# Last context rows in fp32 over four column groups inside the queries, and a new order of the ramp, in a one-core Perceiver block

## The reference

```python
x = x + xattn(layernorm(x), ctx, ctx, Wq, Wk, Wv, Wo)
# in xattn:
q = (query @ Wq)          # 1024 rows x 1024
k = (key @ Wk)            # 32 x 257 rows x 256
v = (value @ Wv)          # 32 x 257 rows x 256
scores = q @ k.T * 32 ** -0.5          # per batch and head
out = softmax(scores) @ v
return out @ Wo
```

## Time and profile before

| what | us |
|---|---|
| median of three runs | 1087.92 (1085.78 to 1088.8) |
| the profiled execution, and its span | 1086.56, 1085.0 |
| PE busy | 1053.6 (97% of the span) |
| VectorE busy | 631.4 (58%) |
| ScalarE busy | 478.8 (44%) |
| GpSimd busy | 244.4 (23%) |
| first product of the queries starts | 14.09 |
| products of the last context rows, first start | 115.54 |
| first scores start | 140.41 |

### The profile page before, as it was taken

One profiled execution on the slowest core, in us unless ns is written; L12 is line 12 of the kernel. 1 busy time (PEld: TensorE's weight loads), 2 busy tenths in 40 slices (PEclk: granted clock), 3 DMA queues, 4 the chain that ended last, 5 costly groups with the idle time before them and its releaser, 6 DMA issues.

```text
span 1085.0 us, 25336 instructions
## 1 busy us (share of the span) xinstructions
PE 1053.6 (97%) x9020; PEld 962.6 (89%) x9021; DVE 631.4 (58%) x1624; ACT 478.8 (44%) x1129; POOL 244.4 (23%) x414
## 2 busy tenths in 40 slices
PE   9999999999999999999999999799998899999996
PEld 8999889999999999999999999577776778888885
DVE  6641256666667666666666677577878444354220
ACT  4321245555555555555545555533324244454331
POOL 2000211211212121212111121044464222322232
PEclk9999999999999999999999999899999999999998
DMA  9442567575757565675657664465538587588332
GB/s 342 138 155 81 185 188 195 169 205 159 208 149 210 164 191 163 191 185 175 191 176 204 209 177 130 146 222 93 106 100 265 160 241 252 141 254 255 102 76 37
DMA packets 78602, 189.45 MB, mean 175 GB/s; under 512 B 16512, under 2 KB 27136, under 8 KB 74400
## 3 DMA queue, kind: packets, MB, share of 16 engines
q1 hardware_dynamic: 64096, 154.15, 46.3%
q0 software_dynamic: 14400, 33.88, 13.2%
HBM read 148.66 MB, written 44.56 MB: 178 GB/s over the span
## 4 chain that ended last, share of the span: by engine, by line
PE 88%; DMA 4%; DVE 3%; issue 2%; POOL 1%; ACT 1%; POOLq 0%; SPq 0%; DVEq 0%; ACTq 0%
PE bank L1694 17%; PE bank L711 16%; PE bank L720 16%; PE bank L672 9%; PE bank L1540 6%; PE bank L759 6%; PE bank L703 5%; PE bank L778 4%; PE bank L844 3%; DMA xg<-n_scratch,idx 1%; PE bank L1601 1%; PE bank L1574 1%; DMA out_x<-acc,idx 1%; PE bank L748 1%; PE bank L665 1%
## 5 line engine op out<-in xcount | busy, mean ns | idle before, releaser
L483 ACT ACTIVATE prob<-bank,nmax 128x257 f32<-128x257 f32 x256 | 122.1, 477 | 242.3 <-DVE nmax L629 242.3
L629 DVE TENSOR_REDUCE nmax<-bank 128x1 f32<-128x257 f32 x256 | 108.9, 425 | 158.3 <-PE bank L844 158.3
L720 PE MATMUL bank<-wkv_h,cT_h 128*128 128x256 f32 x512 | 154.5, 302 | 0.0
L711 PE MATMUL bank<-cT_h,wkv_h 128*128 128x256 f32 x512 | 154.2, 301 | 0.0
L720 PE MATMUL bank<-wkv_h,cT_l 128*128 128x256 f32 x512 | 144.6, 282 | 0.0
L711 PE MATMUL bank<-cT_h,wkv_l 128*128 128x256 f32 x512 | 144.2, 282 | 0.0
L720 PE MATMUL bank<-wkv_l,cT_h 128*128 128x256 f32 x512 | 144.1, 282 | 0.0
L711 PE MATMUL bank<-cT_l,wkv_h 128*128 128x256 f32 x512 | 143.9, 281 | 0.0
L377 POOL DMA_DIRECT2D qcat<-q_scratch x128 | 70.5, 557 | 270.9 <-PE bank L844 267.8
L1694 PE MATMUL bank<-w_h,rows_h 128*128 x272 | 108.7, 400 | 0.0
L1694 PE MATMUL bank<-w_l,rows_h 128*128 x272 | 107.3, 394 | 0.0
(11 more groups left out here) (218 smaller groups left out, 2394.6 us busy)
## 6 DMA issues: line engine op xcount, KB each, us to landing
kcat<-k_scratch SPq DMA_DIRECT2D x128, 258.0 KB, 4.3
cx<-in_context SPq DMA_DIRECT2D x32, 1024.0 KB, 7.0
raw<-in_expert_w SPq DMA_DIRECT2D x48, 512.0 KB, 7.6
qcat<-q_scratch POOLq DMA_DIRECT2D x128, 128.0 KB, 3.3
k_scratch<-kT_h SPq DMA_DIRECT2D x32, 258.0 KB, 2.9
k_scratch<-kT_l SPq DMA_DIRECT2D x32, 258.0 KB, 3.1
x_in<-in_x SPq DMA_DIRECT2D x16, 512.0 KB, 8.0
expert_raw<-in_expert_w SPq DMA_DIRECT2D x16, 512.0 KB, 7.9
```

What stands on the lines that cost most here:

```text
L483: act.activation(prob[1 - par][:, s, 0:SK], s_ps[s % 2][:, 0:SK], ACT.Exp, bias=nmax[:, 1 - par, s:s + 1], accum_out=sums[:, 1 - par, s:s ...
L629: dve.reduce_max(nmax[:, 1 - par, s:s + 1], s_ps[s % 2][:, 0:SK], AXX, negate=True).then_inc(max_done, 1)
L711: o = pe.matmul(k_ps[:, j * 256:(j + 1) * 256], wkv[w][:, k, j * P:(j + 1) * P], cT[t][:, b % 2, k, :], start=(j == 0 and k == 0 and n == ...
L720: o = pe.matmul(v_ps[:, a * KV:(a + 1) * KV], cT[t][:, b % 2, k, a * P:(a + 1) * P], wkv[w][:, k, KV:2 * KV], start=(a == 0 and k == 0 and ...
```

## The change

Four places. First, the start: the order of VectorE, ScalarE and PE for the first two tiles of x, and the number of filler turns. Second, the last context rows: the product is done in plain fp32 from `clT` [128 x 8 x 32] and `wkv_raw`, chunk by chunk, with the 512 columns of Wk and Wv in four pieces of 128, each into its own 32 partitions of one bank. It stands between units (3, 0) and (3, 1) of the queries, its turn of the keys between (3, 1) and (3, 2). The first two contexts then wait for this product. Third, behind the queries: the first keys stand directly behind the turns of context 0. Fourth, SP's list: the eight stores of the last values come in front of the third store of queries, the fourth store of queries comes behind the kcat loads of b = 0. ScalarE waits for the stores before it writes `oT` over them.

```diff
@@ -192,7 +192,7 @@
         xn = sh.at("xn", extra + 40 * KB, [P, 2, D])
-        clT = [sh.at("clT_" + part, extra + i * 4 * KB, [P, KC, P], F32R) for i, part in enumerate("hl")]
+        clT = sh.at("clT", extra + 52 * KB, [P, KC, B])
@@ -212,7 +212,7 @@
 
-        kvl = sb("kvl", [B, 2 * KV], F32)
+        kvl = sb("kvl", [P, P], F32)
@@ -224,7 +224,7 @@
         q_ps = lambda n: banks[2 + n % 6]
-        kvl_ps, klT_ps = banks[7], banks[6]
+        clT_ps, klT_ps, kvl_ps = banks[0][:, 0:KC * B], banks[0][:, KC * B:KC * B + 2 * B], banks[1][:, 0:P]
@@ -238,7 +238,7 @@
         q_stored = [sem("q_stored0"), sem("q_stored1")]
@@ -302,14 +302,20 @@
             sp.wait_ge(wkv_l_ready, KC)
+            sp.wait_ge(kvl_done, 1)
...
                 sp.dma_start(cx[:, b, :, :].rearrange("p a n -> p (a n)"), context_rows(context, b)).then_inc(cx_loaded[b], 16)
-            store_q(2)
-            store_q(3)
...
             for s in range(NG):
-                sp.dma_start(vlast_dram[:, s, slot_cols(s)], kvl[:, KV + s * DH:KV + (s + 1) * DH]).then_inc(vl_placed, 16)
+                rows = slice((2 + s // 4) * B, (3 + s // 4) * B)
+                sp.dma_start(vlast_dram[:, s, slot_cols(s)], kvl[rows, slot_cols(s % 4)]).then_inc(vl_placed, 16)
+            store_q(2)
+
+            def load_context(b):
+                if b + 2 < B:
+                    sp.wait_ge(cT_done, 4 * b + 4)
+                    sp.dma_start(cx[:, b % 2, :, :].rearrange("p a n -> p (a n)"), context_rows(context, b + 2)).then_inc(cx_loaded[b % 2], 16)
@@ -319,9 +325,7 @@
                         load_wo(c)
-                if b + 2 < B:
-                    sp.wait_ge(cT_done, 4 * b + 4)
-                    sp.dma_start(cx[:, par, :, :].rearrange("p a n -> p (a n)"), context_rows(context, b + 2)).then_inc(cx_loaded[par], 16)
+                load_context(b)
@@ -333,6 +337,8 @@
                                      k_dram[part, par].rearrange("(g d) n -> d g n", g=4)).then_inc(kcat_loaded[par], 16)
+                if b == 0:
+                    store_q(3)
@@ -358,9 +364,6 @@
                 norm.on_gpsimd(pool, t)
-            pool.wait_ge(q_done, 3 * UNITS)
-            for part in range(2):
-                pool.memset(clT[part][:, :, :].bitcast(F32), 0.0).then_inc(clT_zeroed, 1)
@@ -438,9 +441,8 @@
             x_high(0)
-            wq_high(1)
             x_high(1)
-            wq_high(2, 3, 4, 5, 6, 7)
+            wq_high(1, 2, 3, 4, 5, 6, 7)
@@ -456,17 +458,17 @@
             q_high(2, 2, 3)
-            q_high(3, 0, 1)
-            act.wait_ge(clT_zeroed, 2)
             act.wait_ge(clT_done, 1)
-            act.activation(clT[0][:, :, 0:B], xT_ps(0)[0][:, 0:KC * B].rearrange("p (k b) -> p k b", b=B), ACT.Copy).then_inc(clT_h_ready, 1)
+            act.activation(clT[:, :, :].rearrange("p k b -> p (k b)"), clT_ps, ACT.Copy).then_inc(clT_copied, 1)
+            q_high(3, 0)
+            act.wait_ge(kvl_done, 1)
+            act.activation(kvl[:, :], kvl_ps, ACT.Copy).then_inc(kvl_copied, 1)
+            q_high(3, 1)
+            act.wait_ge(klT_done, 1)
+            act.activation(kl[0][:, :, :].rearrange("p j b -> p (j b)"), klT_ps, ACT.Copy).then_inc(kl_h_ready, 1)
...
                 context_high(0, m)
-            act.wait_ge(kvl_done, 1)
-            act.activation(kvl[:, :], kvl_ps[0:B, :], ACT.Copy).then_inc(kvl_copied, 1)
-            act.wait_ge(klT_done, 1)
-            act.activation(kl[0][:, :, :].rearrange("p j b -> p (j b)"), klT_ps[:, 0:2 * B], ACT.Copy).then_inc(kl_h_ready, 1)
@@ -495,6 +497,8 @@
                         act.wait_ge(pv_done, b - 1)
+                        if (b - 2) % (NT // 2 * BT) == 0:
+                            act.wait_ge(q_stored[(b - 2) // (NT // 2 * BT)], 64)
@@ -526,9 +530,9 @@
 
-            def x_low(t):
+            def x_low(t, *some):
                 g = t // 2
-                for h in range(2):
+                for h in some or range(2):
@@ -562,12 +566,13 @@
             statistics(0)
+            statistics(1)
             normalized(0)
-            statistics(1)
+            normalized(1)
             wq_low(0)
-            normalized(1)
-            x_low(0)
-            x_low(1)
+            for h in range(2):
+                for t in range(2):
+                    x_low(t, h)
@@ -602,15 +607,12 @@
             q_low(3, 0, 1)
-            dve.wait_ge(clT_h_ready, 1)
-            dve.tensor_tensor(clT[1][:, :, 0:B], xT_ps(0)[0][:, 0:KC * B].rearrange("p (k b) -> p k b", b=B),
-                              clT[0][:, :, 0:B].bitcast(F32), ALU.subtract).then_inc(clT_l_ready, 1)
+            dve.wait_ge(kl_h_ready, 1)
+            dve.tensor_tensor(kl[1][:, :, :].rearrange("p j b -> p (j b)"), klT_ps,
+                              kl[0][:, :, :].rearrange("p j b -> p (j b)").bitcast(F32), ALU.subtract).then_inc(kl_l_ready, 1)
...
                 context_low(0, m)
-            dve.wait_ge(kl_h_ready, 1)
-            dve.tensor_tensor(kl[1][:, :, :].rearrange("p j b -> p (j b)"), klT_ps[:, 0:2 * B],
-                              kl[0][:, :, :].rearrange("p j b -> p (j b)").bitcast(F32), ALU.subtract).then_inc(kl_l_ready, 1)
@@ -678,7 +680,7 @@
                     if k % 4 == 0:
-                        pe.wait_ge(xT_l_ready, 3 + k // 4)
+                        pe.wait_ge(xT_l_ready, 2 + k // 4 * 2)
@@ -785,11 +787,11 @@
             pe.wait_ge(ident_ready, 1)
-            keep_busy(38)
+            keep_busy(32)
             turn_x(0)
-            keep_busy(16)
+            keep_busy(4)
             turn_x(1)
-            keep_busy(8)
+            keep_busy(10)
@@ -805,29 +807,33 @@
             queries(2, 2, 3)
-            queries(3, 0, 1)
...
             for k in range(KC):
-                o = pe.transpose(xT_ps(0)[0][:, k * B:(k + 1) * B], cl[:, k * P:(k + 1) * P], ident[0:B, 0:B])
+                o = pe.transpose(clT_ps[:, k * B:(k + 1) * B], cl[:, k * P:(k + 1) * P], ident[0:B, 0:B])
             o.then_inc(clT_done, 1)
+            queries(3, 0)
+            pe.wait_ge(clT_copied, 1)
+            for n in range(2):
+                pe.wait_ge(wkv_loaded[n], 16)
+            for k in range(KC):
+                for g in range(4):
+                    o = pe.matmul(kvl_ps[g * B:(g + 1) * B, :], clT[:, k, :], wkv_raw[:, k, g * P:(g + 1) * P],
+                                  start=(k == 0), stop=(k == KC - 1), skip_group_check=True)
+            o.then_inc(kvl_done, 1)
+            queries(3, 1)
+            pe.wait_ge(kvl_copied, 1)
+            pe.transpose(klT_ps, kvl[0:2 * B, :], ident[0:2 * B, 0:2 * B]).then_inc(klT_done, 1)
             queries(3, 2, 3)
-            pe.wait_ge(clT_l_ready, 1)
+            pe.wait_ge(kl_l_ready, 1)
...
             pe.wait_ge(wkv_l_ready, KC)
-            for k in range(KC):
-                for n, (t, w) in enumerate(PASSES):
-                    o = pe.matmul(kvl_ps[:, :], clT[t][:, k, :], wkv[w][:, k, :], start=(k == 0 and n == 0), stop=(k == KC - 1 and n == 2))
-            o.then_inc(kvl_done, 1)
-            pe.wait_ge(cT_l_ready, 4)
+            pe.wait_ge(cT_l_ready, 2)
...
                 keys(0, 0, first)
-            pe.wait_ge(kvl_copied, 1)
-            for j in range(2):
-                o = pe.transpose(klT_ps[:, j * B:(j + 1) * B], kvl[:, j * P:(j + 1) * P], ident[0:B, 0:B])
-            o.then_inc(klT_done, 1)
+            pe.wait_ge(cT_l_ready, 4)
```

More of the change, by code:

```diff
@@ L240, in attend @@
         q_stored = [sem("q_stored0"), sem("q_stored1")]
-        clT_zeroed, clT_done, clT_h_ready, clT_l_ready = sem("clT_zeroed"), sem("clT_done"), sem("clT_h_ready"), sem("clT_l_ready")
+        clT_done, clT_copied = sem("clT_done"), sem("clT_copied")
         kvl_done, kvl_copied, klT_done, kl_h_ready, kl_l_ready = (
```

## The result

The changed kernel takes 1079.09 us, median of five executions (1076.48 to 1081.28); the kernel before took 1085.78 beside it (1085.28 to 1088.8). The ratio is 0.9923, interval 0.9908 to 0.9938: 8.4 us less (6.7 to 10.0). The profiled execution took 1080.17 against 1086.56, 6.4 less.

What follows compares the result with a forecast made beforehand. PE, busy 97% of the span, was taken to bound the kernel. -1.95 + 2.1 + 0.3 - 5.65 - 2.0 + 0.5 = -6.7 us, from 1086.56 to 1079.9 us (1081.2 against the median); range 1078.5 to 1085.

Steps and rivals of the forecast that it cites:

- Start: Start of the kernel: the first product of the queries begins at 12.15 instead of 14.09 us, 1.95 us less.
- rival 1: First queries: the clock is at 1.2 GHz there, costing 1 to 3 us, total 1083 us; chance 0.16.
- Product in column groups: Inside the queries: the last context rows' fp32 product adds 2.1 us, its one transpose 0.3 us.
- Rival 2: Product inside the queries: its column groups don't overlap, 5.8 us more, total 1087 us; chance 0.03.
- Behind the queries: After the queries: context 1's turns start at 117.2 instead of 122.87 us, 5.65 us less.
- rival 3: Fourth store of queries shares DMA engines with step 0's kcat, then holds step 1's key stores; 1095 us, chance 0.05.
- The wait for kcat: First scores: PE's wait for kcat falls from 2.22 to about 0.2 us, 2.0 us less.
- A new wait at the second scores: Second scores: kcat of step 1 comes 1.5 us later, making a new wait of 0.5 us.
- The sum: Whole kernel: all terms together make 6.7 us less, 1079.9 us against the profiled 1086.56; chance 0.66.
- Rival 4: Later in the kernel: half or all of the 6.7 us is given back, 1084.5 to 1088 us; chance 0.10.

Runs made afterwards that it cites:

- all but the start: The kernel before with every edit of the change except those of the start; ratio 0.993 (0.9907 to 0.9952) against the kernel before.
- no filler: The changed kernel without any filler turn; ratio 0.9914 (0.9891 to 0.9937) against the kernel before.
- context 0 first: The changed kernel with context 0's first two turns split by ScalarE and VectorE before the last unit of queries; ratio 0.9917 against the kernel before.

## Why the prediction was right or wrong

- **Start, -1.95.** -2.07 (14.09 to 12.02). GpSimd's step started 0.18 us behind the normalization, took 0.66 us and ended 0.08 us behind it, as I took it. In the profile of all but the start the step got in 0.1 us before the weights' product on VectorE and took 0.22 us; then its neighbour L135 took 1.46 us instead of 0.57 and ended 0.43 us behind that product. The Trainium skill, SBUF — State Buffer, in the part on the shared port pair, says that the pair is an exclusive lock, held for a whole instruction by the one that starts first; both traces agree with it.
- **The clock at the start (rival 1).** Did not come. The clock rose at 4.7 to 5.9 us in the changed kernel's three profiles and, without any filler, at 11.9. Transposes alone raised it in all of them. The Trainium skill, TensorE: Matmul & The Clock Gate, in the part on the PE-mode transpose, says that they don't count as busy in the same way; these traces do not bear it out. My idle times were wrong: I let 32 turns end near 6.7, but 38 took 6.84 us from 1.77 on the earlier trace rows, so 32 end near 7.9 with the six at the dense end of the row taken off at 0.11 us each (an estimate from the 1.91 us of 16 dense turns). They ended at 7.30, and PE then stood 1.0 us in all, not 2.4.
- **Product in column groups, +2.1 and +0.3.** 2.07 and 0.4. Rival 2 is excluded by the exchanged loops, where the groups don't overlap and the product takes 5.95 us.
- **Behind the queries, -5.65.** -5.67. What I left out is that this also brings the key stores closer to the transfers in front of them; see rival 3.
- **The wait for kcat, -2.0. This is the step that failed.** In the profile at hand it was -1.55 (2.22 to 0.67, within its bounds). But I took 2.22 as the price of the place, and gave the place no clock. Four profiles of before have 2.2 to 4.0, mean 3.05, and two of them another 1.5 us in step 1 for the low clock behind it. The changed kernel has 0.4 in the mean and none. That is 2.6 and 0.8 instead of 2.0. I had the mechanism (the values' stores in front of the third context, that in front of the key stores) but not that transfers queued that closely scatter by 2 us. The change makes the scatter smaller and does not end it: with the changed queue, the profiles of all but the start and of no filler waited 1.72 each, and their high keys' stores took 3.5 and 4.4 us where those of the changed kernel took 2.6 to 3.3.
- **A new wait at the second scores, +0.5.** 0 in all three profiles of the changed kernel (step 1 took 15.98 to 16.00). The kcat loads of step 1 were issued 9.0 us behind the first scores (142.58), where they were issued 8.1 behind them before (148.56); I had forecast 1.5 later, it was 0.9, and there was 1 us to spare. It appeared as 0.36 when the first scores came earlier (context 0 first), and as 0.5 in the profile of all but the start.
- **Rival 3.** Did not come, but its mirror image is what the fourth store did in its old place. I priced this move as a possible loss of 0 to 2 us and counted no gain for it; without it the kernel loses about 6 us. It is the second half of the failed step: I asked what the store would delay in its new place, and not what it would delay in its old one once the third context moved forward to it and the key stores came 5 us earlier. The forecast named the price of an empty queue without saying that this move is what empties it.
- **The sum.** With the measured terms, -2.07 + 2.47 - 5.67 - 1.55 = -6.8 at the first scores, where 6.85 were found. With the mean wait and clock, -2.07 + 2.47 - 5.67 - 2.6 - 0.8 = -8.7; from the means over profiles, the second scores moved from 158.0 to 149.4, 8.6 us, where I had forecast 6.7. That the first two profiles differ by 6.4, near the forecast, was luck: the one of before has the shortest wait of the four.
- **Rival 4.** It came in part, and I gave it 0.10. From the second scores to the last ones of the block nothing is lost (539.5 to 542.0 us in the seven profiles of the kernel before and its variants, 539.0 to 542.3 in the eleven of the changed kernel and its variants). From the last scores to the end the seven took 385.0 to 388.6 us, mean 386.6, and the eleven 387.1 to 389.9, mean 388.7: 2.0 us lost again. They are lost near 850 us, around the wait of PE for the first rows of x that a DMA gathers for the experts. It is 1.3 to 2.5 us in the seven and 0.3 to 4.5 in the eleven, and behind the longer waits the turns run slower (8 of them in 1.97 us instead of 1.09). The first profile of before and the second of the changed kernel:

```profile
856.24 1.09 PE L1601 MATMUL bank<-ident,xg 128*128 128x128 f32 x8 [1.47 <-DMA xg<-n_scratch,idx]
```

```profile
849.53 1.97 PE L1607 MATMUL bank<-ident,xg 128*128 128x128 f32 x8 [4.50 <-DMA xg<-n_scratch,idx]
```

The edits don't touch this part, and why the wait differs stays open.
- **What stays open in the total.** By the spans of the profiles, the kernel went from 1086.0 (mean of four) to 1078.8 (mean of three), 7.2 us: 8.6 won by the second scores, less what is lost late. The timed comparisons say 8.4 and 10.0. The profiles don't account for that difference of 1 to 3 us, and so the 8.6 at the second scores must not be taken as the explanation of the ratios. The median of the kernel before was 1085.8 to 1090.3 in the comparisons here; what makes the chips or hours differ was not tried.

## What to carry to other kernels

When a wait ends on a DMA that is queued closely behind others, one profile shows one value out of a spread: take several profiles, and add what the engine's clock does when it comes out of the wait. When a transfer is moved, price both places with everything else already moved; the gain of one move can hang on the other. A gain at one place is compared with the whole time only after the rest of the kernel has been compared too: here 2 us were lost again 700 us later. Four column groups in turn made these fp32 products three times cheaper than the same products group by group.

## What the runs showed of the hardware

- A key store of 258 KB landed 2.2 to 3.3 us after its issue where the third context had gone out 7.5 to 13 us in front of it (3.5 and 4.4 for the high keys in two such profiles), and took 4.7 to 7.3 where 1 MB had gone out 1.2 to 3.4 us in front of it on the same queue, or 3 MB 7.5 to 9.4 us in front.
- Waits of PE at the first scores of 3.37 to 4.96 us were followed by 1.2 GHz in all five profiles that have them, for 3.4 us in four and 6.8 in one; waits of 0 to 2.62 us kept 2.4 GHz in the other twelve, and so did 3.7 us with turns in them. 3.4 us of low clock made step 1 1.5 us longer, 6.8 made it 2.4 longer.
- fp32 transposes of 128 x 128 alone raised the clock in every profile; 16 of them took 3.65 us from an idle start, 8 take 1.09 once it is up.
- fp32 products of 32 weight columns by 128: 60 ns apart in alternating column groups, 186 ns in the same one. The Trainium skill, TensorE: Matmul & The Clock Gate, part on packing small matmuls, gives 2.38 times for three column tiles of 512 columns; here it is 3.1 times for four of 128.
- SP took 0.35 to 0.43 us to issue the load of a context (1 MB) by itself, 0.55 and 0.83 right behind two stores of 1 MB, and 3.4 to 4.2 behind four kcat loads and two such stores.
